# First layer of a two-layer transformer kernel: row minima begun head by head, waits of the scores by head, statistics moved two slots, VectorE and ScalarE orders rewritten

## What is computed

```python
h = _layernorm(x, axis=-1) * (1 + ca) + sa
x = x + ga * _L0_attn_ref(h, ...)      # 16 heads of 16 channels, causal, ALiBi distances, softmax, output projection
h = _layernorm(x, axis=-1) * (1 + cb) + sb
x = x + gb * _L0_ffn_ref(h, ...)       # time mix with the token before: sigmoid(xr Wr) * (relu(xk Wk)^2 Wv)
```

## Time and profile before

| | us |
|---|---|
| median of 3 runs (3446.08 to 3448.98) | 3448.22 |
| the profiled execution, its own time | 3447.82 |
| span of the profile, first to last instruction | 3445.8 |
| the 32 slots, from the first scores to the last AV | 678 |

### The profile page before, as it was taken

One profiled execution on the slowest core, in us unless ns is written; L12 is line 12 of the kernel. 1 busy time (PEld: TensorE's weight loads), 2 busy tenths in 40 slices (PEclk: granted clock), 3 DMA queues, 4 the chain that ended last, 5 costly groups with the idle time before them and its releaser, 6 DMA issues. The chain is left out here.

```text
span 3445.8 us, 47573 instructions
## 1 busy us (share of the span) xinstructions
PE 3037.0 (88%) x18084; PEld 2080.5 (60%) x18084; DVE 1743.6 (51%) x5089; ACT 1368.4 (40%) x2965; POOL 852.7 (25%) x833
## 2 busy tenths in 40 slices
PE   5788888876899999999999999999998688769993
PEld 2566666653656565666666666666666334468883
DVE  2566666653555544444444444446564466741114
ACT  2666555541344444443434343434343121112222
POOL 1000011002232322222222222233333100105554
PEclk7989999887899999999999999999999899659996
DMA  4000000003000000000000000000000000112325
GB/s 128 15 17 16 17 17 17 14 3 147 7 7 4 10 15 27 1 1 1 11 30 1 1 1 1 28 14 10 6 10 5 10 0 0 59 40 72 77 79 171
DMA packets 65114, 93.60 MB, mean 27 GB/s; under 512 B 9931, under 2 KB 52942, under 8 KB 63848
## 3 DMA queue, kind: packets, MB, share of 16 engines
q1 hardware_dynamic: 57208, 74.24, 7.4%
q0 software_dynamic: 7680, 16.32, 1.9%
HBM read 59.31 MB, written 27.36 MB: 25 GB/s over the span
## 5 line engine op out<-in xcount | busy, mean ns | idle before, releaser
L1376 PE MATMUL bank<-h2T,w 128*128 128x512 f32 x1024 | 484.0, 606 | 12.6 <-ACT h2T L1281 12.6
L1408 PE MATMUL bank<-w,gT 128*128 128x256 f32 x2048 | 464.4, 380 | 0.0
L1408 PEld LDWEIGHTS bank<-w,gT 128*128 128x128 f32 x2048 | 379.5, 190 | 46.9 <-issue 0.5
L1047 POOL TENSOR_TENSOR prob<-prob,rsum 128x512 f32<-128x512 f32 (+1 forms) x256 | 237.8, 949 | 651.4 <-DVE rsum L1199 651.4
L1316 ACT ACTIVATE gT<-bank,vec 128x512 f32<-128x512 f32 x256 | 175.2, 687 | 331.4 <-PE bank L1376 331.0
L1376 PEld LDWEIGHTS bank<-h2T,w 128*128 128x128 f32 x1024 | 180.2, 190 | 198.9 <-issue 181.1
L628 ACT ACTIVATE y<-y,least 128x128 f32<-128x128 f32 (+3 forms) x512 | 247.9, 553 | 53.3 <-DVE least L516 53.3
L1205 DVE COPY probT<-bank 128x1024 f32<-128x1024 f32 (+1 forms) x128 | 139.1, 1087 | 241.4 <-PE bank L1424 241.4
L1290 ACT ACTIVATE prob<-prob,least 128x256 f32<-128x256 f32 (+1 forms) x512 | 239.6, 470 | 17.3 <-DVE least L1171 16.9
L516 DVE CUSTOM_DVE_ANT_0 y<-bank,mask 128x128 f32<-128x128 f32 (+3 forms) x512 | 220.1, 484 | 27.7 <-PE bank L716 26.7
L1351 PE MATMUL bank<-wtok,hT 128*128 128x512 f32 x512 | 226.9, 596 | 1.0 <-ACT hT L1281 1.0
(11 more groups left out here) (289 smaller groups left out, 5358.8 us busy)
## 6 DMA issues: line engine op xcount, KB each, us to landing
w<-in_W SPq DMA_DIRECT2D x8, 1024.0 KB, 5.5
expert_parts<-zeros SPq DMA_DIRECT2D x8, 1024.0 KB, 15.7
we<-in_we SPq DMA_DIRECT2D x16, 512.0 KB, 5.2
rows<-modulation SPq DMA_DIRECT2D x40, 128.0 KB, 3.0
x<-in_x SPq DMA_DIRECT2D x8, 512.0 KB, 9.7
prob<-score SPq DMA_DIRECT2D x64, 64.0 KB, 2.4
probT<-score SPq DMA_DIRECT2D x64, 64.0 KB, 2.4
y<-expert_parts SPq DMA_DIRECT2D x8, 512.0 KB, 8.8
```

The lines of the kernel that those rows point to most:

```text
L1047: nc.gpsimd.tensor_tensor(two, two, rsum[:, at:at + 2].unsqueeze(2).to_broadcast([P, 2, width]), ALU.mult).then_inc(s["probs"], 1)
L1376: ins = nc.tensor.matmul(M[m % 2][:, :], w1[:, k, m * P:(m + 1) * P], h2T[:, k, :], start=(k == 0), stop=(k == KD - 1))
L1408: ins = nc.tensor.matmul(M[i][:, (t % 2) * D:(t % 2 + 1) * D], gT[:, m, t * P:(t + 1) * P], w2[:, m, :], start=(m == 0), stop=(m == MF - 1))
```

## The change

The waits and the hand-written orders of three engines change; no arithmetic, buffer or instruction is added or taken away, and TensorE's order of products is the same.

```diff
+def turn_of(tile, head):
+    return [k for k, (t, j0, nj) in enumerate(TURNED) if t == tile and j0 <= head < j0 + nj][0]
...
@@ GpSimd
-                if q == 1 and b + 2 < B:
+                if q == 2 and b + 2 < B:
                     rstd(b + 2)
@@ VectorE: shifted
-                if n:
-                    upto = 1 + max(k for k, x in enumerate(TURNED) if x[0] == tile)
-                    dve.wait_ge(s["pt_full0"], PTS * (n - 1) + upto)
                 dve.wait_ge(s["scores_full"], 3 * n + u + 1)
                 for j in heads:
+                    if n:
+                        dve.wait_ge(s["pt_full0"], PTS * (n - 1) + 1 + turn_of(tile, j))
@@ VectorE: order of a slot
                 turned(m, (0,))
+                if live:
+                    shifted(n, 0, 0, (0, 1))
                 for f in side["norm"]:
                     norm(f, ...)
                 taken(parts[0])
                 turned(m, (2,))
-                taken(parts[1])
-                if live:
-                    shifted(n, 0, 0, (0, 1))
-                turned(m, (4,))
                 if live:
                     shifted(n, 0, 0, (2, 3))
+                if q == 2 and b + 2 < B:
+                    stats(b + 2)
+                taken(parts[1])
+                turned(m, (4,))
                 taken(parts[2])
+                if live:
+                    shifted(n, 1, 0, (0, 1))
                 turned(m, (6,))
                 if live:
-                    shifted(n, 1, 0, range(4))
+                    shifted(n, 1, 0, (2, 3))
+                    shifted(n, 1, 1, range(4))
                 taken(parts[3])
-                if q == 1 and b + 2 < B:
-                    stats(b + 2)
-                if live:
-                    shifted(n, 1, 1, range(4))
                 turned(m, (9,))
-                taken(parts[4])
                 if live:
                     shifted(n, 2, 0, range(4))
-                if q == 1 and b + 2 < B:
+                taken(parts[4])
+                if q == 2 and b + 2 < B:
                     norm(b + 2, ...)
@@ ScalarE: order of a slot
                 taken(parts[0])
+                if live:
+                    exps(n, 0, 0, (0, 1))
                 turned(m, (3,))
                 taken(parts[1])
                 if live:
-                    exps(n, 0, 0, (0, 1))
+                    exps(n, 0, 0, (2, 3))
                 turned(m, (5,))
+                taken(parts[2])
                 if live:
-                    exps(n, 0, 0, (2, 3))
-                taken(parts[2])
-                turned(m, (7, 8))
+                    exps(n, 1, 0, (0, 1))
+                turned(m, (7,))
                 if live:
-                    exps(n, 1, 0, range(4))
+                    exps(n, 1, 0, (2, 3))
+                turned(m, (8,))
                 taken(parts[3])
...
                 taken(parts[4])
-                taken(parts[5])
                 if live:
                     exps(n, 2, 0, range(4))
+                taken(parts[5])
@@ TensorE: scores
-                pe.wait_ge(s["least0"], 16 * n + (0, 4, 12)[u])
-                for tile, at in UNITS[u]:
+                before = 16 * n + (-4, 0, 8)[u]
+                for i, (tile, at) in enumerate(UNITS[u]):
                     for j in range(4):
+                        if i == 0 and before >= 0:
+                            pe.wait_ge(s["least0"], before + j + 1)
```

## The result

The changed kernel takes 3366.55 us (median of 4 runs, 3365.23 to 3375.24) against 3447.85 us (4 runs, 3446.08 to 3448.98): a ratio of 0.9771, 95% interval 0.9756 to 0.9786. That is 81 us less, where 62 were forecast; it lies 1.6 us above the lower edge of the forecast's range, 3365.

What follows compares the result with a forecast made beforehand. TensorE was taken to bound the kernel, losing time idle and to a lowered clock. Gains of 57.7 and 18.2 us less 13.7 for the clock gave 62.2 us, from 3448.2 to 3386 us, range 3365 to 3405 (chance 0.62).

Steps and rivals of the forecast that it cites:

- What bounds the kernel: First-layer slots: TensorE sets the pace, losing time idle (scores wait 74.7 us for least values) and to a 0.90 clock.
- The replay of the slots: Slots replayed at full clock from row durations: a sequence's four slots take 77.8 us against 88.9, 11.1 us less.
- Turn 8, turn 10, L2, AV: New TensorE waits: turn 8 0.55 us more; turn 10 0.8 in q = 0, early up to 1.6; L2 0.6; AV 1.8.
- Moved statistics: 1.8 us of statistics and 1.4 of norm move to q = 2 and hide in VectorE's waits for turns.
- Waits by head on TensorE: Heads 0 to 2 of the scores may start early, but turns then wait one by one; net nothing.
- The sum: Sequences 2 to 6 gain 57.7 us, the others 18.2, less 13.7 for low-clock stretches: 62.2 us faster.
- the quarter: Sequences 0, 1 and 7: a quarter of their 72.7 us recoverable time is gained, 18.2 us.
- a clock term: One low-clock stretch in each of eight sequences costs 1.7 us, 13.7 us in all.
- A: Rival: many new short waits at turn 8 and AV keep the granted clock at 0.92; 3428 us, chance 0.18.
- B: Rival: the new waits don't appear, since VectorE and ScalarE run ahead of the replay; 3347 us, chance 0.10.
- C: Rival: ScalarE's turn copies stand behind exponentials, which wait for VectorE, which waits for TensorE; slower, 3460 us, chance 0.05.
- D: Rival: the second and third scores wait just as long for something else; time as before, 3448 us, chance 0.05.

## Why the prediction was right, and where its sizes were off

*What bounds the kernel.* Right: idle time at the scores and the clock behind it. Both came back, 37 us of the one and 41 us of busy time through the other.

*The replay of the slots.* Right within half a microsecond: 18.9, 20.7, 19.2 and 19.0 us forecast for q = 0 to 3, 18.95, 20.25, 19.19 and 19.03 measured; 77.8 for a full sequence, 77.42 measured.

*Turn 8, turn 10, L2, AV.* All four new waits came. Turn 8 waits 0.92 us (0.41 + 0.55 forecast), turn 10 in q = 0 0.59 (0.8), L2 0.36 (0.6), AV 1.57 (1.8). In the first sequences turn 10 waits 0.90 us, where up to 1.6 were forecast. Against the earlier trace rows, the waits of the scores in q = 0 are gone.

*Moved statistics.* Right: the slot with q = 2 is 19.19 us, with VectorE busy 13.59 us where it was 12.15 (1.4 more, where I had said 3). The statistics and the norm did bring 1.40 + 0.38 + 1.38 us into that slot; but in the kernel before, a `mixT` instruction of the slot with q = 1 reached 2.4 us into it, and it now ends in q = 1. With the statistics back, 21.5 us are lost.

*Waits by head on TensorE.* Right: 1 us, inside the noise. What the text did not say plainly is that the same waits on VectorE were a condition of the replay (head 0 read by 3.0 us, before turn 3 exists). The kernel with tile waits puts 102 us on that.

*The sum.* For sequences 2 to 6 it had 57.7 us less 5 stretches at half clock, 49.2; measured are 12.2 + 11.5 + 9.9 + 11.5 + 11.9 = 57.0, with one such stretch, in sequence 4 (79.05 against 77.42: 1.6 us, for which 1.7 was the forecast). For sequences 0, 1 and 7, which I gave a quarter of their recoverable time less three stretches, 18.2 - 5.1 = 13.1, it is 3.6 + 6.7 + 11.5 = 21.8. The slots gave 78.8 us in all, the rest of the program, for which I had nothing, about 2.5.

*The terms that were mis-sized.* So 19 us are missing from the sum: 8 in sequences 2 to 6, 9 in sequences 0, 1 and 7, and 2.5 outside the slots. In sequences 2 to 6 it is the clock: one stretch, not five. In the others it is the quarter, a guess that no row carried; 12.6 of their 21.8 us are idle time (8.1 of it in sequence 7) and 9.2 busy time. The clock as a whole was not mis-sized: read as in the prediction, length times the share below full clock, the changed kernel still loses 8.3 us in sequence 0, 1.6 in sequence 4 and 5.1 in sequence 7, 15 us where 13.7 were put down. It lies in three sequences, and none is in the other five. That the total agrees is luck, and so is it that the sum without a clock term, 75.9 us or 3372, is only 5 us off. The range held with 1.6 us to spare, though three terms erred the same way. The Trainium skill (TensorE: Matmul & The Clock Gate, "What's actually happening") says that activity releases the throttle. The trace agrees in the five sequences at 1.00, but not with what I made of it in the prediction, that no low stretch would remain with short waits only: the one in sequence 4 follows a wait of 1.57 us.

*The rivals.* A is out: the clock went to 0.97. B, no new waits, is out: they are all there, and about 20 us were left in them. C, a ring of VectorE, ScalarE and TensorE, did not decide this change: the turns wait 13.7 us in all for ScalarE's copies. A milder form shows in the kernel with only VectorE's copy moved, where these waits are 43.4 us and the time 37 us longer, most of it through the clock. The kernel with tile waits, slower than before, is no case of it: there the turns wait for VectorE (85.2 us) and not for ScalarE (6.4 us). D is out: the second and third scores of a full sequence no longer wait for anything.

## What to carry to other kernels

In kernels with orders written by hand, look for an engine that waits idle in its queue for one thing while another, long finished, stands behind it: its place in the queue is the cost, not its busy time. One move of that kind (65 us alone), and one that took 3 us of other work out of the slot where it stood in the way (17 us alone), gave all of this change's gain; the other reorderings, on VectorE and ScalarE, moved waits from one product to another. When an instruction is moved ahead in such a queue, check that its own wait is as narrow as its data (here a head, not a tile), because everything behind it now waits too.

## What the runs showed of the hardware that I had not expected

Stretches at half clock also follow short waits that stand close together, and not each time. In the kernel with only VectorE's copy moved, the waits of 0.41, 0.92 and 0.86 us in q = 0, with short transposes between them, were followed by matmuls at half speed in sequence 3 (3.78 us for the product above). In sequences 4, 5 and 6 the same waits were followed by full speed. Sequence 4:

```profile
401.85 0.63 PE L740 MATMUL bank<-ident,y 128*128 128x128 f32 x4 [0.93 <-ACT probT L380]
403.35 0.63 PE L740 MATMUL bank<-ident,y 128*128 128x128 f32 x4 [0.86 <-ACT probT L380]
404.55 1.99 PE L783 MATMUL bank<-wf,mixT 128*128 128x256 f32 x8
```

In the changed kernel it is the same with AV's wait in q = 1: 1.57 us was followed by an AV of 2.39 us in sequences 3, 5, 6 and 7, and in sequence 4 by one of 4.01 us, at a granted clock of 0.51, though the slots before it were alike:

```profile
396.07 4.01 PE L754 MATMUL bank<-probT,vt 128*32 128x128 f32 x80 [1.57 <-DVE y L535]
396.00:399.50 3.50, 3.43 (x68) 3.18 (x72) 3.25 (x7) 0.10 (x1) 0.00 (x0) 0.51 0.02 7
```

What decides between the two is not shown by any run here. So a forecast can give such a stretch (1.7 us) only a chance, and a variant that leaves many short waits may gain or lose several of them.
